# A graph layer on one core: the last 64 features' products made whole-array beside zeros, the mask product dropped, the order tables redrawn

## The chip, the core and the metric

The kernel runs on one core of a Trainium2 chip, in one launch. The metric is the device time in microseconds (us). Five engines each work through a list of their own, in order, and meet by semaphores: TensorE (PE) makes matrix products into eight PSUM banks, VectorE (DVE) and ScalarE (ACT) read PSUM, GpSimd (POOL) works in SBUF alone, and SyncE (SP) issues DMAs.

## What is computed

128 graphs of 128 nodes with 64 features. Layer 0, the costly one, sums over each node's neighbours a ReLU of 192 hidden features; layer 1 is a dense message and gate step. Both end in a layer norm.

```
mask = (adj > 0)                                  # 128 graphs, 128 x 128
xj_proj = x @ W1a
h = relu(xj_proj[:, :, None, :] + (x[:, :, None, :] - x[:, None, :, :]) @ W1b + b1)
hm = einsum('bjkh,bjk->bjh', h, mask)             # 192 hidden features
x = layernorm(x + hm @ W2 + deg * b2)             # layer 0
m = relu(relu(x @ W1g + b1g) @ W2g + b2g)
msg = relu(adj @ m)
r, z, n = gates(msg @ W_ih, x @ W_hh)
x = layernorm(x + (1 - z) * n + z * x)            # layer 1
```

## The kernel before

The mask is sparse, about one neighbour in ten. A node's neighbours are taken one after the other, in up to 18 places. Four graphs are one quad; there are 32 quads, q = 0 to 31. For a quad the features of the nodes, projected, lie in three PSUM banks as running pre-activations: banks 0 and 1 hold hidden features 0 to 127 of the four graphs, bank 2 holds features 128 to 191 of two graphs above each other, 64 partitions each. One round moves every node from its present neighbour to the next: PE adds the difference by a product of V (the neighbours' features, fp16, as stationary operand: VA for the first half of the sources, VB for the second) with a step matrix of -1, 0 and 1 in 8 bits (DM, columns = nodes), and DVE then adds the ReLU of the three banks to the sum AC in one SCALAR_TENSOR_TENSOR. A quad has nine rounds on VA (A1 to A9, PE's `round_a`, DVE's L1154) and nine on VB (B1 to B9, `round_b`, DVE's L1174). Rounds 1 to 6 cover 192 columns a graph, 7 and 8 cover 128, 9 covers 80. Places that a node does not use would count the ReLU of its last state too often; the surplus (NNB) that the start value is multiplied with takes that out.

Time step t runs the A rounds of quad t and the B rounds of quad t - 1 in turn: B1, A1, B2, A2, ... B9, A9. A and B use different banks (0 to 2 and 3 to 5), so PE can prepare one while DVE reads the other. A round is eight products on PE: four whole-array ones (`wide`, L841, stationary 128 x 128) and four with 64 stationary columns (`paired`, L850), of which those for partitions 0 to 63 and 64 to 127 run beside each other. `round_b` does `paired` first, `round_a` does `wide` first. B1 also has "leave", the closing product of the A rounds.

Everything else of the kernel is cut into pieces and put between the rounds by hand. The pieces are: p, the preparation of quad t + 1 (`ov`, `rank_t` L749, `rank_ov` L757 to L767, `words` L1120, `x_turn` L780, `v` L792 to L798, `v_low` L804, `v_out` with its DMAs L1777, `surplus` L813 and L816); r, the ranks of a group of eight graphs (`mask` L1688, `rank_n` L728, `split_x`, `count` L1584 to L1603, `off` L735 and, on DVE, SI L1111); t, the tail of quad t - 2 (`s_ov` L912, `out0` L923 to L941); n, d and e, the steps of layer 1 of a group (L609 to L712; its second product m2 is L655 and L658). s are the seeds (L827 and L833, then ACT's `ini` L1517 and POOL's start value, L1735, for which A1 waits), 0 to 3 the unpacking of step matrices on DVE (L1130), c clears AC. The tables ORDER (steps 1 to 30, one row for even and one for odd t), FIRST (t = 0) and LAST (t = 31, 32) say which pieces stand behind which round: a row has 19 places, place 0 ahead of B1, then one behind each B round and one behind each A round. All engines follow the same tables, each with its share of a piece. POOL waits at an unpacking until DVE has done it before it goes on with what stands behind it in the table. The pieces other than rounds use banks 6 and 7 in turn.

Counting of places (`count`) is done by POOL, from the ends of the ranks: NV, N12 = 6 NV and NVC. `surplus` adds on PE the column sums of the mask (L813) and NVC, transposed by a product with the identity (L816).

## Time and profile before

| | us |
|---|---|
| median of 3 runs (899.65 to 905.23) | 900.1 |
| the profiled execution | 907.5 |
| its span, first to last instruction | 905.7 |
| mean granted TensorE clock in it | 0.97 |

| engine | busy us | share | instructions |
|---|---|---|---|
| PE | 818.9 | 90% | 10240 |
| DVE | 795.6 | 88% | 880 |
| ACT | 622.5 | 69% | 1863 |
| POOL | 455.0 | 50% | 534 |

The span is the time from the first to the last instruction of one profiled execution; the runs are timed without the profiler. PE's busy time is the union of its products, whose ends are modelled, so it is not PE at its peak. An fp32 product stands in the trace as two, so L658 x8 are four products of the program. In the timeline a row merges equal instructions that follow each other (x4), its time is from the first's start to the last's end, and what stands in brackets is how long the engine was idle before it and what ended that. DVE's instructions overlap the next one's start a little. The chain that ended last runs over PE for 61% and DVE for 11% of the span.

### The profile page before, as it was taken

The page shows a single profiled execution, that of the slowest core. Times are in us where ns is not written, and L with a number is a line of the kernel's source. Part 1 is how long each engine was busy: PE and PEld are TensorE (multiplying, and loading weights), DVE is VectorE, ACT ScalarE, POOL GpSimd, SP SyncE. Part 2 cuts the span into 40 slices and gives each one's busy share as a digit, 9 for nine tenths or more (in the row PEclk, how much of TensorE's full clock was granted, in tenths as well). Part 3 has the DMA queues.
Part 4 walks back from the last instruction along what each step waited for, and adds up shares of the span by engine and source line. Part 5 has one row for each costly group of instructions (what it writes and reads, how often), then busy time and mean ns, then how long its engine had stood idle before and what let it go on. Part 6 is the DMA issues. An engine that isn't in the chain of part 4 may idle for free.

```text
span 905.7 us, 25602 instructions
## 1 busy us (share of the span) xinstructions
PE 818.9 (90%) x10240; PEld 563.5 (62%) x10240; DVE 795.6 (88%) x880; ACT 622.5 (69%) x1863; POOL 455.0 (50%) x534
## 2 busy tenths in 40 slices
PE   3778989999999999999999999989999999989963
PEld 2446657666676757666676756666675766666642
DVE  5789989999999999999999989999999999978742
ACT  4624557686877868686876868687786868667651
POOL 4413133564737465564736465472746556353751
...
GB/s 128 86 73 49 82 20 48 84 48 77 49 94 31 75 55 48 96 44 81 48 95 19 69 74 49 90 35 94 44 66 52 49 94 48 43 48 31 1 13 25
DMA packets 31564, 53.35 MB, mean 59 GB/s; under 512 B 8273, under 2 KB 17105, under 8 KB 31441
## 3 DMA queue, kind: packets, MB, share of 16 engines
...
q14 instruction: 42, 0.34, 0.1%
...
## 4 chain that ended last, share of the span: by engine, by line
PE 61%; issue 14%; DVE 11%; SPq 4%; DMA 3%; POOL 3%; ACT 2%; POOLq 0%; DVEq 0%
PE PS L841 16%; PE PS L850 11%; DVE AC L1174 5%; PE PS L924 4%; DVE AC L1154 3%; PE PS L912 2%; DMA VB<-VN 2%; PE PS L934 2%; DVE DM L1130 2%; PE PS L658 2%; PE PS L827 2%; PE PS L669 2%; PE PS L609 1%; POOL AC L1735 1%; PE PS L618 1%
## 5 line engine op out<-in xcount | busy, mean ns | idle before, releaser
L1174 DVE SCALAR_TENSOR_TENSOR AC<-PS,AC 128x1152 f32<-128x1152 f32 (+2 forms) x279 | 330.5, 1185 | 33.2 <-PE PS L841 30.9
L1154 DVE SCALAR_TENSOR_TENSOR AC<-PS,AC 128x1152 f32<-128x1152 f32 (+2 forms) x279 | 330.7, 1185 | 30.5 <-PE PS L850 24.9
L841 PE MATMUL PS<-DM,VA 128*128 128x192 fp8e5 (+1 forms) x1024 | 122.1, 243 | 20.1 <-DVE AC L1154 11.6
L841 PE MATMUL PS<-DM,VB 128*128 128x192 fp8e5 (+1 forms) x1024 | 123.6, 244 | 0.5 <-DVE AC L1171 0.5
L1735 POOL TENSOR_TENSOR AC<-AC,NNB 128x512 f32<-128x512 f32 x64 | 63.7, 1015 | 97.0 <-ACT AC L1517 84.4
L841 PEld LDWEIGHTS PS<-DM,VA 128*128 128x128 f16 x1024 | 77.5, 100 | 46.3 <-DVE AC L1154 34.3
L850 PE MATMUL PS<-DM,VB 128*64 128x192 fp8e5 (+1 forms) x1024 | 86.8, 248 | 21.3 <-DVE AC L1174 20.0
L841 PEld LDWEIGHTS PS<-DM,VB 128*128 128x128 f16 x1024 | 68.8, 98 | 35.0 <-issue 1.2
L850 PE MATMUL PS<-DM,VA 128*64 128x192 fp8e5 (+1 forms) x1024 | 88.6, 254 | 0.1
L1130 DVE TENSOR_SCALAR DM<-CW 128x1536 uint16<-128x1536 uint16 (+1 forms) x132 | 80.1, 655 | 3.4 <-DMA CW<-WM 3.4
L850 PEld LDWEIGHTS PS<-DM,VB 128*64 128x64 f16 x1024 | 41.9, 109 | 60.8 <-issue 34.0
L1688 POOL TENSOR_SCALAR MT<-AT 128x1024 bf16<-128x1024 f32 x15 | 41.9, 2794 | 72.0 <-DVE DM L1130 52.3
L1487 ACT ACTIVATE XE<-PS 128x512 f16<-128x512 f32 x64 | 37.8, 592 | 38.4 <-PE PS L781 38.4
L850 PEld LDWEIGHTS PS<-DM,VA 128*64 128x64 f16 x1024 | 36.3, 108 | 37.7 <-issue 30.5
L1728 POOL MEMSET AC<- 128x768 f32 x32 | 23.6, 738 | 71.8 <-PE PS L941 71.2
L1467 ACT ACTIVATE AM<-PS 64x512 int16<-64x512 f32 x64 | 37.9, 592 | 21.4 <-PE PS L749 21.0
L1724 POOL TENSOR_TENSOR SHL<-SO,SHL 128x256 f16<-128x256 f32 x31 | 20.9, 674 | 54.0 <-ACT SHL L1525 53.9
L1493 ACT ACTIVATE VN<-PS 128x384 f16<-128x384 f32 x64 | 31.1, 485 | 22.5 <-PE PS L798 22.5
L924 PE MATMUL PS<-w2s,AC 128*128 128x64 f32 x256 | 41.1, 293 | 0.0
L1498 ACT ACTIVATE VN<-PS 128x384 f16<-128x384 f32 x64 | 31.3, 490 | 13.9 <-PE PS L804 13.9
L912 PE MATMUL PS<-w2s,AC 128*64 128x64 f32 x1024 | 37.6, 228 | 0.0
L924 PEld LDWEIGHTS PS<-w2s,AC 128*128 128x128 f32 x256 | 37.5, 195 | 0.0
...
## 6 DMA issues: line engine op xcount, KB each, us to landing
CW<-WM SPq DMA_DIRECT2D x128, 160.0 KB, 2.8
...
VA<-VN SPq DMA_DIRECT2D x64, 96.0 KB, 2.2
VB<-VN SPq DMA_DIRECT2D x64, 96.0 KB, 2.2
...
```

Source lines behind the costliest of these rows:

```text
L841: last = e.matmul(PS[:, b + i % 2, 256 * (i // 2) + cols.start:256 * (i // 2) + cols.stop], lhs[:, GRAPH[i], 0:128], d[:, i, :], start=Fal ...
L850: last = e.matmul(PS[h, b + 2, 256 * (i // 2) + cols.start:256 * (i // 2) + cols.stop], lhs[:, GRAPH[i], 128:H], d[:, i, :], start=False, ...
L912: last = e.matmul(PS[64 * h:64 * h + 64, b, 64 * i:64 * i + 64], ac[:, n, c:c + 64], w2s[:, w, :], start=(w == 0), stop=(w > 0))
L924: e.matmul(o, ac[:, i % 2, 256 * (i // 2) + 64:256 * (i // 2) + 192], w2s[:, 0, :], start=False, stop=True, skip_group_check=True)
L1130: e.tensor_scalar(DM[m][:, halves], CW[t % 3][:, halves, first], 6 - 2 * m, 0xC0C0, ALU.logical_shift_left, ALU.bitwise_and).then_inc(s["d ...
L1154: e.scalar_tensor_tensor(dst, tiles(PS[:, b:b + 3, :])[:, :, cols], 0.0, dst, ALU.max, ALU.add).then_inc(s["sx"], 1)
L1174: e.scalar_tensor_tensor(dst, tiles(PS[:, b:b + 3, :])[:, :, cols], 0.0, dst, ALU.max, ALU.add).then_inc(s["sy"], 1)
L1467: e.activation(graphs(am[k])[:, :, 64 - 64 * h:192 - 64 * h], src[k], ACT.Copy, scale=2.0, bias=-258.0)
L1487: e.activation(XE[q % 4][:, 2 * k:2 * k + 2, :].rearrange("p i n -> p (i n)"), PS[:, b, :], ACT.Copy).then_inc(s["xe"], 1)
L1498: e.activation(VN[q % 2][:, 1, 2 * k:2 * k + 2, :], PS[:, b, :].rearrange("p (a n) -> p a n", a=2)[:, :, 0:H], ACT.Copy).then_inc(s["vl"], 1)
L1688: e.tensor_scalar(MT[g % 3][:], AT[g % NA][:], 0.0, None, ALU.is_gt).then_inc(s["mask"], 1)
L1735: e.tensor_tensor(t[:, h, nat], t[:, h, nat], NNB[q % 2][:, h, :], ALU.mult).then_inc(s["im"], 1)
```

## The change

Three things. First, `paired` becomes `padded`: the stationary operand of the products for the last 64 features is 128 columns wide, 64 of features and 64 of zeros, so the product writes all 128 partitions of the bank and adds zero to the other graph's half. VN, VA and VB get 256 places a graph instead of 192, with zeros behind the 192, set once by POOL; for every second graph the features are stored with the last 64 first, so that `left` and `right` find 128 features, or 64 beside 64 zeros, in a row of memory. For that `v` cuts its products for these graphs in two (64 and 128 columns). The copies of `v` go to every second graph. The DMAs of VA and VB move 128 KB instead of 96. The seeds keep their 64-column products.

Second, `surplus` loses the product over the mask: GpSimd's count takes the number of neighbours from the ends of the ranks, which it has in CT, into NVC, and ACT adds the constant as a bias.

Third, ORDER, FIRST and LAST are new throughout. DVE's and ACT's instructions for a piece are the same as before.

```
-    ("2ps3ee", "t", "", "pp", "", "ed", "dre", "t", "rtpp", "tc", "erdeee", "", "pdr", "p", "e", "pp", "rp", "", "0e1"),
-    ("d2sp3", "pp", "", "t", "dpe", "t", "pe", "pcttn", "n", "lpd", "d", "p", "d", "d0", "d", "p", "rdddp", "", "p1"),
+    ("s2p", "p", "pe3ee", "td", "erp", "t", "tt", "rpr", "p", "ed", "p", "epree", "pee", "d", "pce", "", "", "0", "r1"),
+    ("s2", "p3dp", "t", "", "d", "p", "eptp", "e", "ptl", "tp", "ndcpn", "d", "p", "dr", "pnd", "", "dd", "d", "01p"),
...
+        def left(t, i):
+
+            return t[:, i, 64 * (i % 2):64 * (i % 2) + 128]
+
+        def right(t, i):
+
+            c = 256 * i + 128 - 192 * (i % 2)
+            return t.rearrange("p i n -> p (i n)")[:, c:c + 128]
...
             def v(q, k, b, gates):
+                o = PS[:, b, :].rearrange("p (j n) -> p j n", j=2)
+                pieces = ((0, H, 0),) if k == 0 else ((0, 64, 128), (64, H, 0))
+                for c, d, f in pieces:
+                    e.matmul(o[:, :, c:d], on1[:], br[:, f:f + d - c].unsqueeze(1).to_broadcast([128, 2, d - c]), start=True, stop=True,
+                             skip_group_check=True)
                 for j in range(2):
                     x = XE[q % 4][:, 2 * j + k, nat]
+                    for w in (wxh, wxl):
+                        for c, d, f in pieces:
+                            last = e.matmul(o[:, j, c:d], x, w[:, 1, f:f + d - c], start=False, stop=True, skip_group_check=True)
...
             def surplus(q, b, gates):
-                mt = MT[g % 3][:, c:c + 4, :]
-                e.matmul(PS[:, b, :], on1[:], mt.rearrange("p (k a) n -> p a k n", a=2), start=True, stop=False)
                 for i in range(4):
                     m = c + GRAPH[i]
                     last = e.matmul(PS[:, b, 128 * i:128 * i + 128], NVC[g % 2][:, m:m + 1].to_broadcast([128, 128]),
-                                    idb[:], start=False, stop=(i == 3))
+                                    idb[:], start=True, stop=True)
...
-            def paired(q, lhs, d, cols):
+            def padded(q, lhs, d, cols):
 
                 b = 3 * (q % 2)
                 for i in range(4):
-                    h = slice(64 * (i % 2), 64 * (i % 2) + 64)
-                    last = e.matmul(PS[h, b + 2, 256 * (i // 2) + cols.start:256 * (i // 2) + cols.stop],
-                                    lhs[:, GRAPH[i], 128:H], d[:, i, :], start=False, stop=True, skip_group_check=True)
+                    last = e.matmul(PS[:, b + 2, 256 * (i // 2) + cols.start:256 * (i // 2) + cols.stop],
+                                    right(lhs, i), d[:, i, :], start=False, stop=True, skip_group_check=True)
...
-                e.activation(nnb[:, 0:512], PS[:, b, :], ACT.Copy)
+                e.activation(nnb[:, 0:512], PS[:, b, :], ACT.Copy, bias=-2.0 * C0)
...
-                e.tensor_tensor(NVC[i][:], cs[:, CSL + 1:CSL + 2].to_broadcast([128, GB]), N12[i][:, :, 0], ALU.subtract).then_inc(s["nvc"], 1)
+                e.tensor_tensor(CT[:], CT[:], N12[i][:], ALU.subtract).then_inc(s["nvc"], 1)
                 en.wait_ge(s["nvc"], 2 * g + 1)
-                e.tensor_tensor(NVC[i][:], NVC[i][:], N12[i][:, :, 1], ALU.subtract).then_inc(s["nvc"], 1)
+                e.tensor_tensor(NVC[i][:], CT[:, :, 0], CT[:, :, 1], ALU.add).then_inc(s["nvc"], 1)
...
             def setup():
+                for t in VN:
+                    e.memset(t[:].rearrange("p h i n -> p (h i) n")[:, :, H:256], 0.0)
```

What the tables do is best seen in the engines' lists. On PE, at the boundary of an even step to an odd one (t = 10 to 11), behind the last A9 product, before (L813 and L816 surplus, L655 and L658 m2, L827 and L833 seeds, L742 ov, then leave and B1):

```order
L813 MATMUL PS<-MT,on 128x512
L816 MATMUL PS<-idb,NVC 128x128 x4
L655 MATMUL PS<-br,on 128x512
L658 MATMUL PS<-BD,M 128x128 x4
L827 MATMUL PS<-XE,wxh 128x256 x4
L827 MATMUL PS<-XE,wxl 128x256 x4
L833 MATMUL PS<-XE,wxh 64x256 x4
L833 MATMUL PS<-XE,wxl 64x256 x4
L742 MATMUL PS<-SI,shf 128x512
L841 MATMUL PS<-CW,VA 128x128 x4
L850 MATMUL PS<-CW,VA 64x128 x4
L850 MATMUL PS<-DM,VB 64x192 x4
```

The same place in the changed kernel (there L850 is `wide` and L858 is `padded`, L743 is off, L825 surplus, L836 and L842 the seeds, L750 ov, L663 and L666 m2):

```order
L743 MATMUL PS<-NV,tri 128x16
L825 MATMUL PS<-idb,NVC 128x128 x4
L836 MATMUL PS<-XE,wxh 128x256 x4
L836 MATMUL PS<-XE,wxl 128x256 x4
L842 MATMUL PS<-XE,wxh 64x256 x4
L842 MATMUL PS<-XE,wxl 64x256 x4
L850 MATMUL PS<-CW,VA 128x128 x4
L858 MATMUL PS<-CW,VA 128x128 x4
L858 MATMUL PS<-DM,VB 128x192 x4
L850 MATMUL PS<-DM,VB 128x192 x4
L750 MATMUL PS<-SI,shf 128x512
L663 MATMUL PS<-br,on 128x512
```

The mask product is gone, m2 and ov have moved behind B1, off has come to stand ahead of the surplus, and only the seeds still change the tiling.

On DVE at the same boundary, from B9 to A1, before (L1174 are B rounds, L1154 A rounds, L1130 the unpacking; SI, L1111, is ahead of B9):

```order
L1111 TENSOR_TENSOR SI<-iot,VE 128x1024
L1174 SCALAR_TENSOR_TENSOR AC<-PS,AC 128x6x80
L1154 SCALAR_TENSOR_TENSOR AC<-PS,AC 128x6x80
L1130 TENSOR_SCALAR DM<-CW 128x1536 x4
L1174 SCALAR_TENSOR_TENSOR AC<-PS,AC 128x6x192
L1154 SCALAR_TENSOR_TENSOR AC<-PS,AC 128x6x192
```

And now (L1182 are B rounds, L1162 A rounds, L1138 the unpacking, L1119 SI):

```order
L1182 SCALAR_TENSOR_TENSOR AC<-PS,AC 128x6x80
L1138 TENSOR_SCALAR DM<-CW 128x1536
L1162 SCALAR_TENSOR_TENSOR AC<-PS,AC 128x6x80
L1119 TENSOR_TENSOR SI<-iot,VE 128x1024
L1138 TENSOR_SCALAR DM<-CW 128x1536 x2
L1182 SCALAR_TENSOR_TENSOR AC<-PS,AC 128x6x192
L1138 TENSOR_SCALAR DM<-CW 128x1536
L1162 SCALAR_TENSOR_TENSOR AC<-PS,AC 128x6x192
```

SI has moved behind A9, and the four unpackings are spread from B9 to A1.

## Rows read from the trace of the kernel before

**Rows 1.** Windows, one pair of steps: length, each engine's busy time, clock, DMA.

```profile
409.02:460.29 51.27, 49.27 (x640) 34.15 (x639) 47.94 (x47) 39.21 (x119) 28.99 (x34) 1.00 0.24 63
```

**Rows 2.** Waits of DVE, 100 to 790 us: total, times, longest.

```profile
DVE AC L1174 <- PE PS L841: 22.9, 39, 1.3
DVE AC L1154 <- PE PS L850: 19.7, 48, 1.7
```

**Rows 3.** Timeline of DVE at two boundaries: start, us, what, idle before it.

```profile
406.06 1.96 DVE L1130 TENSOR_SCALAR DM<-CW 128x1536 uint16<-128x1536 uint16 x4
409.02 1.36 DVE L1174 SCALAR_TENSOR_TENSOR AC<-PS,AC 128x1152 f32<-128x1152 f32 x1 [1.00 <-PE PS L841]
410.67 1.36 DVE L1154 SCALAR_TENSOR_TENSOR AC<-PS,AC 128x1152 f32<-128x1152 f32 x1 [0.29 <-PE PS L850]
...
431.46 2.56 DVE L1130 TENSOR_SCALAR DM<-CW 128x1536 uint16<-128x1536 uint16 x3
434.29 1.36 DVE L1174 SCALAR_TENSOR_TENSOR AC<-PS,AC 128x1152 f32<-128x1152 f32 x1 [0.26 <-PE PS L841]
436.20 1.36 DVE L1154 SCALAR_TENSOR_TENSOR AC<-PS,AC 128x1152 f32<-128x1152 f32 x1 [0.56 <-POOL AC L1735]
```

**Rows 4.** Timeline of DVE within steps.

```profile
419.51 1.36 DVE L1154 SCALAR_TENSOR_TENSOR AC<-PS,AC 128x1152 f32<-128x1152 f32 x1 [0.43 <-PE PS L850]
...
437.48 1.35 DVE L1174 SCALAR_TENSOR_TENSOR AC<-PS,AC 128x1152 f32<-128x1152 f32 x1
438.74 1.35 DVE L1154 SCALAR_TENSOR_TENSOR AC<-PS,AC 128x1152 f32<-128x1152 f32 x1
...
445.34 0.81 DVE L1120 TENSOR_TENSOR WM<-c,AM 128x1280 uint16<-128x1280 uint16 x1
...
452.30 0.96 DVE L1154 SCALAR_TENSOR_TENSOR AC<-PS,AC 128x768 f32<-128x768 f32 x1
...
455.07 1.22 DVE L1111 TENSOR_TENSOR SI<-iot,VE 128x1024 bf16<-128x1024 bf16 x1
456.20 0.65 DVE L1174 SCALAR_TENSOR_TENSOR AC<-PS,AC 128x480 f32<-128x480 f32 x1
```

**Rows 5.** Timeline of PE, A1 and B2 of an even step.

```profile
435.26 0.50 PE L841 MATMUL PS<-DM,VA 128*128 128x192 fp8e5 x4
435.70 0.36 PE L850 MATMUL PS<-DM,VA 128*64 128x192 fp8e5 x4
435.89 0.33 PE L850 MATMUL PS<-DM,VB 128*64 128x192 fp8e5 x4
436.15 0.50 PE L841 MATMUL PS<-DM,VB 128*128 128x192 fp8e5 x4
436.49 0.38 PE L749 MATMUL PS<-MT,trt 128*128 128x512 bf16 x1
```

**Rows 6.** Timeline of PE from A9 to B1, boundary of an even to an odd step.

```profile
404.45 0.39 PE L813 MATMUL PS<-MT,on 128*128 128x512 bf16 x1
404.68 0.39 PE L816 MATMUL PS<-idb,NVC 128*128 128x128 bf16 x4
...
406.01 0.60 PE L827 MATMUL PS<-XE,wxh 128*128 128x256 f16 x4
...
408.48 0.50 PE L841 MATMUL PS<-DM,VB 128*128 128x192 fp8e5 x4
```

**Rows 7.** Timeline of POOL, start value of the even step.

```profile
434.10 1.98 POOL L1735 TENSOR_TENSOR AC<-AC,NNB 128x512 f32<-128x512 f32 x2 [0.96 <-DVE DM L1130]
```

**Rows 8.** Timeline of POOL and DVE, start of the kernel.

```profile
8.36 0.72 POOL L1674 TENSOR_SCALAR be<-bs 128x192 f32<-128x192 f32 x1 [4.21 <-DMA bs<-in_b2g]
...
64.52 0.56 DVE L1130 TENSOR_SCALAR DM<-CW 128x1536 uint16<-128x1536 uint16 x1 [0.89 <-DMA CW<-WM]
```

**Rows 9.** The page: a group of weight loads, and the DMAs of VA.

```profile
L841 PEld LDWEIGHTS PS<-DM,VA 128*128 128x128 f16 x1024 | 77.5, 100 | 46.3 <-DVE AC L1154 34.3
VA<-VN SPq DMA_DIRECT2D x64, 96.0 KB, 2.2
```

More of the change, by code:

```diff
@@ L51 @@
 CSL = CIO + 64
-CML = CSL + 2
+CML = CSL + 1
 CMR = CML + 128
@@ L98, in constants @@
     c[:, CSL] = less
-    c[:, CSL + 1] = 2.0 * less - 2.0 * C0
     c[0, CML:CML + 128] = -C1
@@ L255, in build @@
         CW = [sb(f"CW{i}", [128, 2, 1280], U16) for i in range(3)]
-        VN = [sb(f"VN{i}", [128, 2, 4, H], F16) for i in range(2)]
-        VA = [sb(f"VA{i}", [128, 4, H], F16) for i in range(3)]
-        VB = [sb(f"VB{i}", [128, 4, H], F16) for i in range(3)]
+        VN = [sb(f"VN{i}", [128, 2, 4, 256], F16) for i in range(2)]
+        VA = [sb(f"VA{i}", [128, 4, 256], F16) for i in range(3)]
+        VB = [sb(f"VB{i}", [128, 4, 256], F16) for i in range(3)]
         XE = [sb(f"XE{i}", [128, 4, 256], F16) for i in range(4)]
@@ L877, in round_a @@
                     pe.wait_ge(s["sx"], 9 * q + n - 1)
-                last = wide(q, VA[q % 3], d, cols)
+                last = wide(q, VA[q % 3][:], d, cols)
                 if q == 0:
@@ L881, in round_a @@
                     pe.wait_ge(s["sx"], n - 1)
-                paired(q, VA[q % 3], d, cols).then_inc(s["gx"], 1)
+                padded(q, VA[q % 3][:], d, cols).then_inc(s["gx"], 1)
             def round_b(q, n):
@@ L888, in round_b @@
                     leave = lasts(q, 0, 0)
-                    wide(q, VA[q % 3], leave, nat)
-                    paired(q, VA[q % 3], leave, nat)
+                    wide(q, VA[q % 3][:], leave, nat)
+                    padded(q, VA[q % 3][:], leave, nat)
                 elif q == NQ - 1:
@@ L894, in round_b @@
                     pe.wait_ge(s["sy"], 9 * q + n - 1)
-                last = paired(q, VB[q % 3], d, cols)
+                last = padded(q, VB[q % 3][:], d, cols)
                 if q == NQ - 1:
@@ L1504, in surplus @@
                 nnb = NNB[q % 2][:].rearrange("p i n -> p (i n)")
-                e.activation(nnb[:, 0:512], PS[:, b, :], ACT.Copy)
+                e.activation(nnb[:, 0:512], PS[:, b, :], ACT.Copy, bias=-2.0 * C0)
                 for a in range(2):
                     h = slice(64 * a, 64 * a + 64)
-                    last = e.activation(nnb[h, 512:768], PS[h, b, 256 * a:256 * a + 256], ACT.Copy)
+                    last = e.activation(nnb[h, 512:768], PS[h, b, 256 * a:256 * a + 256], ACT.Copy, bias=-2.0 * C0)
                 last.then_inc(s["nnc"], 1)
```

30 lines of the change are left out of this document (13 added, 17 removed).

## The prediction

> **What bounds the kernel now.** I read the windows first. Between about 50 and 850 us the kernel repeats a pair of time steps, an odd one from the B1 at 409.02 to that at 434.29 and an even one to 460.29, 51.27 us together. In it TensorE (PE) is busy 49.27 us and VectorE (DVE) 47.94 [rows 1]: neither is plainly the bound, and PE's busy time is modelled from matmuls that overlap, so it can't be taken at its word. The waits of DVE say more: from 100 to 790 us, 13.5 such pairs, it stood 42.6 us (22.9 + 19.7) for products of PE [rows 2]. The timeline says where: B1 and A1, just behind the step boundary, wait 1.00 and 0.29 us in one step, 0.26 and, for GpSimd (POOL), 0.56 in the other [rows 3]; within a step mostly A4, 0.43 [rows 4]. Other rounds start 1.26 apart, which is what DVE itself needs: 1.35, less 0.09 of overlap [rows 4]. So DVE is to be fed, and PE, which works in order, is late for it at a few places.
>
> What PE's time goes into is seen in its timeline [rows 5]. From four whole-array products of 192 columns to whole-array work it is 0.34 us (436.15 to 436.49), 0.083 each. The same four ahead of 64-column ones take 0.44 (435.26 to 435.70). Four 64-column ones run two beside each other: 0.19 to the next such four, 0.26 to whole-array ones. Each change of tiling costs about 0.10 us, and PE was not waiting there for anything else.
>
> **The change, part by part.** All sums are for one pair of steps; counts are from PE's instruction list.
>
> *Padding.* The paired products become whole-array products beside zeros: four slots a group instead of two. 24 groups of 192 columns add 2 x 0.083 each, 4.0; eight of 128 and the two closing ones (leave) 2 x 0.056, 1.1; four of 80 columns 2 x 0.035, 0.3 (0.056 and 0.035 are 0.083 scaled by columns). That is +5.4 us. Against it the changes of tiling fall from 72 to 14: 58 x 0.10 = -5.8. The product over the mask (L813) goes, 0.23 each (404.45 to 404.68) [rows 6], -0.45. Cutting every second V into 64 + 128 columns adds five instructions a step and no columns, some 0.02. PE's own work goes from 47 to 45.7, hardly more than -1 us. Were half of a switch hidden, it would rise by 1.5 or so instead; I take the full price, since the row shows PE going from one group right to the next.
>
> The Trainium skill, "TensorEngine Tiling (Array Packing)", Key Properties, says that changing the tiling mode drains TensorE, which the 0.10 agrees with. Its Theoretical Speedup gives two 64-column tiles up to 2x, and that speaks against this change: by it alone the pair gets 5.4 us of PE work more, some 78 us in all.
>
> *The order tables.* DVE needs, for a pair, 24 x 1.26 + 8 x 0.87 + 4 x 0.57 for rounds, 8 x 0.48 for unpacking steps (L1130, 1.96 for four [rows 3]), 1.13 for SI and 2 x 0.73 for WM, each its row less the overlap [rows 4]: 46.0. Of the 5.3 us more that it takes, 1.1 is that three L1130 last 2.56 where POOL works, against 1.47 [rows 3]; the rest is waiting. More than 5.3 can't be gained. I go through the pair with the new lists and the rows' durations: a round of 192 columns needs 0.67 on PE, starts 0.05 after DVE frees its bank, and 0.21 pass from its last slot to DVE (B1: 408.48, 0.34 of slots, 409.02 [rows 6]).
>
> Even to odd, zero at B9's end (before: 405.49, the 0.57 of A9 ahead of 406.06). Before, surplus, the m2 products (L655, L658) and a switch stand ahead of the seeds, which begin at 406.01, +0.52 [rows 6]. Now 0.25 us of work does, and seeds begin at +0.05, right behind B9. Seeds 0.87, switch and second part 0.55, switch and leave 0.56, B1 0.67: issued by 2.69, so DVE could start at 2.90. But DVE has B9, A9, SI and three L1130 in its list and comes at 3.13: B1 no longer waits. m2, ov and rank_t (1.54) follow, then A1: DVE has it at 5.10 (0.23 late), one more L1130 done on the way. Before, A1 came 5.18 after B9 [rows 3], with SI outside.
>
> Odd to even: surplus, seeds, ov, leave and B1 are issued by 2.91, DVE starts B1 at 3.12, some 1.1 idle (before 434.29 - 430.89 = 3.40, B9's end again 0.57 ahead of the L1130 at 431.46). A1 follows at 4.39, if its start value is there: before, POOL's two products began 0.96 late behind an L1130 [rows 7] for which the new list no longer holds them, so 5.31 (436.20 - 430.89) - 0.96 = 4.35 is possible.
>
> Between: from A1 to the end of B9 DVE has eleven rounds of 1.26, four of 0.87, B9 0.57 and WM 0.73, 18.7. Odd step: A1's issue ends at 4.89, the s_ov products 0.93, two switches and B2 0.67 make 6.70, DVE 6.91 against 6.37: 0.53 late. In the same way A3, B6, A6 and B8 are late by 0.08, 0.10, 0.04 and 0.30. A4 is not, as its 1.24 of fillers are split between A3 and B5. So 5.10 + 18.7 + 1.05 = 24.9. Even step: the fourth L1130 stands here, nothing is late: 4.39 + 18.7 + 0.48 = 23.6. Together 48.5; fp32 fillers ran about 0.1 over their slots and there are three: 48.8. The pair goes from 51.3 to 48.8, **-2.5 us**. Steps 2 to 30 are 14.5 pairs: -36. Later pairs of before ran 0.25 longer than this one on average, from A1's waits; half of that, -2.
>
> *Taken as nothing.* Two memsets of VN on POOL (about 0.5 each, an estimate from the zeroing of others of that size) lie ahead of 4.21 us in which POOL waits for the biases [rows 8]; without that cover, 1. VA and VB grow by a third: 2.2 us to landing [rows 9] may become 2.9, but v_out is issued a round (1.76) earlier; uncovered, 0.7 a step, 20. GpSimd's counting has nine instructions before and after, ScalarE's bias adds none. *Start:* step 1 stood 0.89 for a CW behind 30 weight loads on SP's queue [rows 8]; that L1130 now comes after A9: -1. Last two steps: 0, within 3, since their tables are new and a chain of layer-1 work that the change leaves alone ends the kernel.
>
> Sum: -39. The profiled run took 907.5 us (span 905.7), so 868.5; the median of the runs shown is 7.4 lower, which gives **861 us**.
>
> **Rivals.** *The start value sets A1.* ScalarE's two copies and POOL's two products lie between seeds and A1. If A1 of the even step stays 5.3 behind B9, 0.9 a pair is lost: 1.6 x 14.5 = 23, 875 with start and later pairs. For it: the 0.56 wait [rows 3]. Against: 0.96 of it is a hold that goes. 0.16. *Nearly all waiting goes:* 47.7 a pair, so -52: 847. It needs two engines with 45.7 and 46.0 us of work to interlock almost without loss. 0.11. *Padded weight loads show:* LDWEIGHTS takes 0.1 [rows 9]; at that pitch all padded products add 3.8 a pair, PE needs 49.5, 1.5 is gained: 878. Against: the whole-array groups load the same 128 columns at 0.083. 0.03. The Trainium skill, "TensorE: Matmul & The Clock Gate", Back-to-back issue gap, has about 81 ns for load and product of 128 columns; here even 192 columns take 0.083. *No change:* a late round only moves, as each group waits for the round before; under 0.6 a pair: 893 to 905. 0.06. *Slower, the count ahead of the seeds:* L743 waits for nv from POOL and now stands ahead of surplus, seeds, leave and B1, where L735 stood before B9. DVE's SI needs it too. By the boundary above some 3 us late cost nothing, 5.5 eat the gain; with three more stretches of POOL's work like that of [rows 7] (5.9) and their handovers in front, 0.7 a pair is lost: 910. Against: POOL's list has the same work between mask and count as before. 0.04.
>
> **Chances.** Forecast 0.60 (850 to 872), then 0.16, 0.11, 0.03, 0.06, 0.04. The range 845 to 884 leaves out the last two and tails. Within 1% (9 us) the runs of this kernel (899.65 to 905.23) hardly tell a change from none. Faster by over 1%: 0.60 + 0.16 + 0.11 + 0.03 = 0.90; within 0.06; slower 0.04.
>
> **What would show it.** A pair of 48.8 (47.7 to 50); groups of padded products 0.34 apart and 14 changes of tiling; no wait at B1 of odd steps, about 1.0 at B1 of even ones, 0.5 at B2 of odd ones. Wrong if padded groups take more, if A1 waits for L1735, if PE waits at L743 or L757, or if L1130 lasts over 1 us again.

## The result, and the profile after the change

| | before | after |
|---|---|---|
| median, us | 901.3 (899.65 to 905.23, 4 runs) | 877.9 (874.1 to 877.97, 4 runs) |
| ratio, with its 95% interval | | 0.9724 (0.9681 to 0.9767) |
| the profiled execution: time, span | 907.5, 905.7 | 877.9, 876.3 |

The kernel is 2.8% faster, by about 25 us. The forecast was 861 us with a range of 845 to 884: the sign and the range hold, and the size, 40 us, was put too high by about 15.

A pair of steps in the trace of the changed kernel, an odd step from the B1 at 398.37 to that at 423.69 and an even one to 448.35, shows what became of [rows 1]. The columns are the window, its length, each engine's busy time with its instructions, the granted clock, and the DMA share and rate.

```profile
core 0: us, PE busy (x) PEld busy (x) DVE busy (x) ACT busy (x) POOL busy (x), PEclk, DMA share, GB/s
398.37:423.69 25.32, 25.16 (x331) 20.95 (x332) 23.51 (x25) 18.77 (x58) 11.19 (x10) 1.00 0.33 90
423.69:448.35 24.66, 22.75 (x316) 19.12 (x316) 24.66 (x25) 19.31 (x61) 18.20 (x25) 1.00 0.21 50
398.37:448.35 49.98, 47.91 (x646) 40.07 (x648) 48.17 (x49) 38.08 (x119) 29.39 (x34) 1.00 0.27 70
```

The pair went from 51.27 to 49.98 us; 48.8 was forecast. The two halves differ: in the odd step PE is busy nearly all the time, in the even one DVE is. Next come DVE's waits from 100 to 790 us. Before the change it waited 42.6 us for PE there [rows 2], and 4.2 more for POOL, by the first line; the other three lines are from after the change:

```profile
DVE AC L1154 <- POOL AC L1735: 4.2, 7, 0.9
...
DVE AC L1182 <- PE PS L850: 21.6, 40, 1.0
DVE AC L1162 <- PE PS L858: 0.6, 1, 0.6
DVE AC L1162 <- POOL AC L1745: 0.4, 2, 0.2
```

So 46.8 us of waiting became 22.6: for PE 22.2 instead of 42.6, for POOL 0.4 instead of 4.2. The places are as they should be: the waits at A1, A4 and B9 went. But DVE's own busy time in the pair is 48.17, against 47.94 before. The timeline of DVE (start, duration, what, and idle time before it, where there is some) shows both boundaries from B1 on, and the instruction that grew:

```profile
398.37 1.34 DVE L1182 SCALAR_TENSOR_TENSOR AC<-PS,AC 128x1152 f32<-128x1152 f32 x1
399.64 1.05 DVE L1138 TENSOR_SCALAR DM<-CW 128x1536 uint16<-128x1536 uint16 x1
400.62 1.34 DVE L1162 SCALAR_TENSOR_TENSOR AC<-PS,AC 128x1152 f32<-128x1152 f32 x1
402.32 1.36 DVE L1182 SCALAR_TENSOR_TENSOR AC<-PS,AC 128x1152 f32<-128x1152 f32 x1 [0.36 <-PE PS L850]
...
421.18 1.51 DVE L1138 TENSOR_SCALAR DM<-CW 128x1536 uint16<-128x1536 uint16 x3
423.69 1.36 DVE L1182 SCALAR_TENSOR_TENSOR AC<-PS,AC 128x1152 f32<-128x1152 f32 x1 [0.99 <-PE PS L850]
424.97 1.36 DVE L1162 SCALAR_TENSOR_TENSOR AC<-PS,AC 128x1152 f32<-128x1152 f32 x1
...
427.97 1.35 DVE L1162 SCALAR_TENSOR_TENSOR AC<-PS,AC 128x1152 f32<-128x1152 f32 x1
429.24 1.90 DVE L1128 TENSOR_TENSOR WM<-c,AM 128x1280 uint16<-128x1280 uint16 x1
431.06 1.34 DVE L1182 SCALAR_TENSOR_TENSOR AC<-PS,AC 128x1152 f32<-128x1152 f32 x1
```

B1 and A1 at both boundaries behave as forecast (no wait at B1 of the odd step; 0.99 at that of the even one; none at its A1, where POOL's 0.56 stood in [rows 3]). But the shift that makes WM took 1.90 us, and 0.82 in [rows 4]. What POOL did meanwhile, from its timeline:

```profile
427.83 1.27 POOL L1653 TENSOR_TENSOR GT<-XG,GN 128x512 f32<-128x512 f32 x1 [1.77 <-ACT GN L1403]
429.18 1.27 POOL L1656 TENSOR_TENSOR GT<-GT,GZ 128x512 f32<-128x512 f32 x1
430.42 1.25 POOL L1734 TENSOR_TENSOR SHL<-SO,SHL 128x256 f16<-128x256 f32 x1
```

L1656, a product of layer 1's gate, had begun 0.06 us ahead of WM and runs to 430.45; WM ends at 431.14, 0.69 behind that. L1734, which is next on POOL and takes 0.67 elsewhere (below), takes 1.25 here and ends at 431.67, 0.53 behind WM. From the times it looks as if WM could not go on before POOL's instruction was done, and POOL's next one not before WM was. The rounds, fp32 with one operand in PSUM, keep their 1.35 under such a POOL instruction (the one at 427.97 runs under L1653). Grouped by form over 150 to 770 us (busy time in us and the mean of one in ns stand behind the bar), this is, before:

```profile
L1130 DVE TENSOR_SCALAR DM<-CW 128x1536 uint16<-128x1536 uint16 x99 | 62.3, 682 | 0.0
L1120 DVE TENSOR_TENSOR WM<-c,AM 128x1280 uint16<-128x1280 uint16 x24 | 19.6, 815 | 0.0
```

and after:

```profile
L1138 DVE TENSOR_SCALAR DM<-CW 128x1536 uint16<-128x1536 uint16 x97 | 58.2, 629 | 0.0
L1128 DVE TENSOR_TENSOR WM<-c,AM 128x1280 uint16<-128x1280 uint16 x25 | 32.9, 1315 | 0.0
```

By the means, at equal counts, unpacking gained about 5 us and WM lost about 12: in all 13 even steps in which L1656 runs, WM has met it. The old tables had put WM where POOL was idle. The new ones moved it, for the even steps, from 11.05 us behind B1 (445.34 in [rows 4], B1 at 434.29) to 5.55 (429.24, B1 at 423.69).

### The profile page after: what moved, and what is told of

It is laid out like the page before. It is cut to its first block, busy times and chain, and to the rows that moved or that the text cites. A ratio compares the mean times of both kernels' runs of the same rounds, so it can differ in the third digit from the quotient of the medians.

```text
span 876.3 us, 25828 instructions
## 1 busy us (share of the span) xinstructions
PE 786.3 (90%) x10335; PEld 651.6 (74%) x10368; DVE 803.6 (92%) x880; ACT 606.7 (69%) x1863; POOL 462.1 (53%) x536
## 4 chain that ended last, share of the span: by engine, by line
PE 51%; issue 28%; DVE 16%; ACT 2%; POOL 1%; DMA 1%; SPq 1%; POOLq 0%; DVEq 0%
PE PS L850 12%; PE PS L858 11%; DVE AC L1182 8%; DVE AC L1162 4%; PE PS L836 2%; PE PS L932 2%; PE PS L920 2%; PE PS L677 2%; PE PS L842 2%; PE PS L666 2%; PE PS L617 1%; PE PS L618 1%; PE PS L620 1%; PE PS L629 1%; PE PS L627 1%
## 5 line engine op out<-in xcount | busy, mean ns | idle before, releaser
L1182 DVE SCALAR_TENSOR_TENSOR AC<-PS,AC 128x1152 f32<-128x1152 f32 (+2 forms) x279 | 329.4, 1181 | 26.6 <-PE PS L850 25.1
L1162 DVE SCALAR_TENSOR_TENSOR AC<-PS,AC 128x1152 f32<-128x1152 f32 (+2 forms) x279 | 329.4, 1180 | 4.9 <-PE PS L858 2.9
L850 PE MATMUL PS<-DM,VA 128*128 128x192 fp8e5 (+1 forms) x1024 | 121.5, 241 | 17.2 <-DVE AC L1162 11.1
L858 PE MATMUL PS<-DM,VB 128*128 128x192 fp8e5 (+1 forms) x1024 | 120.6, 240 | 17.9 <-DVE AC L1182 15.0
L850 PE MATMUL PS<-DM,VB 128*128 128x192 fp8e5 (+1 forms) x1024 | 119.8, 240 | 0.5 <-DVE AC L1179 0.5
L858 PE MATMUL PS<-DM,VA 128*128 128x192 fp8e5 (+1 forms) x1024 | 120.3, 240 | 0.1
L850 PEld LDWEIGHTS PS<-DM,VA 128*128 128x128 f16 x1024 | 77.7, 99 | 47.8 <-DVE AC L1162 30.4
L1745 POOL TENSOR_TENSOR AC<-AC,NNB 128x512 f32<-128x512 f32 x64 | 66.1, 1053 | 85.7 <-DVE DM L1138 51.4
L858 PEld LDWEIGHTS PS<-DM,VB 128*128 128x128 f16 x1024 | 75.6, 98 | 43.4 <-issue 18.8
L858 PEld LDWEIGHTS PS<-DM,VA 128*128 128x128 f16 x1024 | 83.5, 98 | 0.9 <-DVE AC L1159 0.6
L850 PEld LDWEIGHTS PS<-DM,VB 128*128 128x128 f16 x1024 | 83.4, 98 | 0.9 <-DVE AC L1179 0.9
L1138 DVE TENSOR_SCALAR DM<-CW 128x1536 uint16<-128x1536 uint16 (+1 forms) x132 | 79.2, 628 | 2.5 <-DMA CW<-WM 2.5
L1738 POOL MEMSET AC<- 128x768 f32 x32 | 23.6, 739 | 66.9 <-PE PS L949 66.2
L1734 POOL TENSOR_TENSOR SHL<-SO,SHL 128x256 f16<-128x256 f32 x31 | 28.5, 918 | 49.7 <-ACT SHL L1533 49.7
L1540 ACT ACTIVATE XR<-PS 128x256 f32<-128x256 f32 x32 | 12.3, 384 | 48.5 <-PE PS L949 48.5
L1430 ACT ACTIVATE YO<-Y,st 128x64 f32<-128x64 f32 x120 | 31.8, 337 | 16.3 <-POOL st L1633 16.3
L1128 DVE TENSOR_TENSOR WM<-c,AM 128x1280 uint16<-128x1280 uint16 x32 | 39.7, 1240 | 2.0 <-ACT OT L1489 2.0
```

The lines of the kernel that those rows point to most:

```text
L850: last = e.matmul(PS[:, b + i % 2, 256 * (i // 2) + cols.start:256 * (i // 2) + cols.stop], left(lhs, i), d[:, i, :], start=False, stop=Tr ...
L858: last = e.matmul(PS[:, b + 2, 256 * (i // 2) + cols.start:256 * (i // 2) + cols.stop], right(lhs, i), d[:, i, :], start=False, stop=True, ...
L1128: e.tensor_tensor(WM[q % 2][:], c7[:], AM[q % 2][:].bitcast(U16), ALU.logical_shift_left).then_inc(s["wm"], 1)
L1138: e.tensor_scalar(DM[m][:, halves], CW[t % 3][:, halves, first], 6 - 2 * m, 0xC0C0, ALU.logical_shift_left, ALU.bitwise_and).then_inc(s["d ...
L1162: e.scalar_tensor_tensor(dst, tiles(PS[:, b:b + 3, :])[:, :, cols], 0.0, dst, ALU.max, ALU.add).then_inc(s["sx"], 1)
L1182: e.scalar_tensor_tensor(dst, tiles(PS[:, b:b + 3, :])[:, :, cols], 0.0, dst, ALU.max, ALU.add).then_inc(s["sy"], 1)
```

## The experiments

All are edits of the changed kernel, run with the kernel before beside them. Step lengths are from B1 to B1 in the timelines, between steps 8 and 27; where no range is given it is the usual length, and in several kernels one to three of these steps are longer, by up to 1.5 us. "Ratio" is to the kernel before.

| kernel | odd step | even step | median us | ratio (95%) |
|---|---|---|---|---|
| before | 25.27 | 26.0 to 27.15 | 901.3 | 1 |
| the change | 25.32 | 24.66 | 877.9 | 0.9724 (0.9681 to 0.9767) |
| e_oldtab | 25.23 | 25.50 to 27.25 | 898.1 | 0.9968 (0.9952 to 0.9985) |
| e_paired | 25.98 | 24.69 | 895.6 | 0.9933 (0.9908 to 0.9957) |
| e_mask | 25.63 | 24.77 | 881.7 | 0.9790 (0.9759 to 0.9820) |
| e_oldlast | 25.31 | 24.65 | 880.3 | 0.9751 (0.9713 to 0.9789) |
| e_words5 | 25.25 | 24.09 | 868.1 | 0.9639 (0.9609 to 0.9669) |
| e_words6 | 25.22 | 24.11 | 870.1 | 0.9642 (0.9607 to 0.9677) |
| e_unpack_even | 25.22 | 24.03 | 870.6 | 0.9651 (0.9618 to 0.9685) |
| e_unpack_both | 25.16 | 24.02 | 869.3 | 0.9647 (0.9613 to 0.9681) |
| e_hold | 25.22 | 24.51 | 874.2 | 0.9691 (0.9656 to 0.9727) |
| e_hold_unpack | 25.22 | 24.44 | 873.0 | 0.9674 (0.9636 to 0.9712) |
| e_hold_paired | 25.92 | 24.64 | 894.4 | 0.9903 (0.9866 to 0.9940) |
| e_gz | 25.29 | 23.96 | 865.7 | 0.9620 (0.9593 to 0.9646) |

### The parts of the change, one at a time

**e_oldtab**: the padded products and the new count under the old tables (ORDER, FIRST and LAST as in the minus lines of the diff).

> The changed kernel (padded products, counting by GpSimd) with all order tables as before the change: what padding and the dropped product are worth without new tables. Theory of the prediction: padding takes 58 changes of tiling of 0.10 us out of a pair of steps and puts 5.4 us of slots in, the product over the mask goes too, so PE has 1 us less work, of which DVE sees at most that: 886 to 898 us, likeliest 892; most of the gain (2.5 us of a pair) is the tables'. Rival, padding itself is the gain: 880 or less. Rival, half of a change of tiling was hidden behind the products, so padding makes PE's work longer: 903 or more.

898.1, 0.3% below the kernel before, at the far end of what the prediction's theory gave. Odd steps stayed at 25.23. In even ones the quiet steps gained 0.5, but some are up to 1.8 longer. The waits of PE, 100 to 790 us, show what goes with it, first before the change, then here:

```profile
PE PS L841 <- DMA VB<-VN: 3.1, 5, 1.2
```

```profile
PE PS L850 <- DMA VB<-VN: 6.5, 6, 1.7
```

With the old tables PE waits now and then for the DMA that brings VB; a third more bytes (128 KB for 96 an issue) and a PE that comes earlier go with the 6.5 us; no run parts the two. Under the new tables, in the change and in e_gz, PE has no such wait from 100 to 790 us. The longer even steps from 20 on of the kernel before (26.32 to 27.15 instead of 26.0, in steps 20 to 28) are these 3.1 us. I had put them down to A1, where they come to light.

**e_paired**: the new tables and count, with the old products.

```diff
-            last = e.matmul(PS[:, b + 2, 256 * (i // 2) + cols.start:256 * (i // 2) + cols.stop],
-                            right(lhs, i), d[:, i, :], ...)
+            h = slice(64 * (i % 2), 64 * (i % 2) + 64)
+            c = 128 - 128 * (i % 2)
+            last = e.matmul(PS[h, b + 2, 256 * (i // 2) + cols.start:256 * (i // 2) + cols.stop],
+                            lhs[:, i, c:c + 64], d[:, i, :], ...)
```

> The changed kernel with the last 64 features' products again as two 64-column products side by side, all else (tables, counting, layout of VA and VB) kept. Theory of the prediction: 5.4 us of slots go and about 58 changes of tiling of 0.10 us come back in a pair, 0.4 more work on PE, and where nothing else stands between rounds the new changes delay a round by 0.05 to 0.1, mostly into waits that DVE has already: 880 to 888 us. Rival, padding is neutral and the tables are all: 876 to 879. Rival, the 64-column pairs win since the changes hide: 870 or less.

895.6: 19 us by the ratios more than the change, and 880 to 888 was expected. Neither half of the change is worth much without the other: the new products and count under the old tables bring 0.3% (e_oldtab), the new tables and count with the old products 0.7%; together they bring 2.8%. Two things are seen in the trace. The odd step is 0.66 longer, 9 us over 14 steps. Rows of PE, A2 of an even step, show why the two forms are so close:

```profile
336.24 0.50 PE L850 MATMUL PS<-DM,VA 128*128 128x192 fp8e5 x4
336.67 0.36 PE L860 MATMUL PS<-DM,VA 128*64 128x192 fp8e5 x4
336.96 0.40 PE L736 MATMUL PS<-trt,MT 128*128 128x128 bf16 x4
```

The whole-array four take 0.43 and the side-by-side four 0.29 to the next, 0.72, and the padded form 0.66 to 0.68 (in the change, from 401.44 to 402.12):

```profile
401.44 0.50 PE L858 MATMUL PS<-DM,VB 128*128 128x192 fp8e5 x4
401.79 0.49 PE L850 MATMUL PS<-DM,VB 128*128 128x192 fp8e5 x4
402.12 0.49 PE L850 MATMUL PS<-DM,VA 128*128 128x192 fp8e5 x4
```

The other is TensorE's clock. Four times between 130 and 820 us it stood at 1.2 GHz (0.50 granted) instead of 2.4 for 3.4 us, as in the second window here:

```profile
350.60:354.00 3.40, 2.49 (x34) 1.40 (x32) 3.40 (x5) 2.27 (x13) 2.57 (x6) 1.00 0.03 8
354.00:357.40 3.40, 3.40 (x27) 2.34 (x29) 3.40 (x6) 2.69 (x9) 0.52 (x1) 0.50 0.64 146
```

The seeds then run at half speed and B1 comes 1.4 to 1.5 late:

```profile
358.94 1.36 DVE L1184 SCALAR_TENSOR_TENSOR AC<-PS,AC 128x1152 f32<-128x1152 f32 x1 [1.37 <-PE PS L850]
```

All four times it was the stretch just ahead of an odd step's B1. Four times 1.4 are 6 us. In the first 130 us, with more such stretches, this execution falls another 5 behind (mean granted clock 0.91 there, 0.96 in the change); but it is the slowest of the ten, 900.6 us, 5 above their median. The mean granted clock of the ten runs was 0.968 to 0.979, that of the change 0.984 to 0.986.

What lowers the clock there is open. Ahead of the fall, in the rounds of 128 and 80 columns, PE had been busy 2.49 of 3.40 us. But it was so at the same place of the nine other boundaries of this kind from step 7 on, where the clock stayed up; the first line below is one of them. And the same place of the change, in the second line, has PE busy for less, 2.34, and the clock up as well:

```profile
299.92:303.32 3.40, 2.49 (x35) 1.40 (x32) 3.40 (x5) 2.27 (x13) 2.57 (x6) 1.00 0.06 13
...
341.57:344.97 3.40, 2.34 (x35) 1.61 (x33) 3.40 (x5) 2.28 (x13) 2.64 (x6) 1.00 0.05 13
```

The Trainium skill, "TensorE: Matmul & The Clock Gate", Part 1, has activity release the throttle. PE's busy time alone does not bear that out here; whether a product on half the columns counts for less than one beside zeros is a guess that no run tests. What the runs show is only that the falls between 130 and 800 us come in the two kernels that have pairs under the new tables, and in none of the padded ones, nor in the kernel before.

**e_mask**: the product over the mask is back in front of surplus, with the old count.

```diff
+                mt = MT[g % 3][:, c:c + 4, :]
+                e.matmul(PS[:, b, :], on1[:], mt.rearrange("p (k a) n -> p a k n", a=2), start=True, stop=False)
...
-                                    idb[:], start=True, stop=True)
+                                    idb[:], start=False, stop=(i == 3))
```

> The changed kernel with the unused places counted as before: the product over the mask (0.23 us on PE) is back in front of the four surplus products, and GpSimd's count and ScalarE's bias are as before the change. Theory of the prediction: surplus stands ahead of the seeds, so B1 of even steps, which waits for PE, comes 0.23 later, and at B1 of odd steps the same 0.23 is about covered by SI and three unpackings on DVE; 0.23 to 0.4 a pair, so 880 to 883 us. Rival, the product was covered: 876 to 878. Rival, GpSimd's new count was what set something: under 874.

881.7, in the range of the prediction's theory. The product is 0.23 us on PE, twice a pair, and the pair is 0.42 longer: both land nearly in full on the path. The even step's B1 now waits 1.23 (0.99 in the change at the same step):

```profile
424.13 1.36 DVE L1185 SCALAR_TENSOR_TENSOR AC<-PS,AC 128x1152 f32<-128x1152 f32 x1 [1.23 <-PE PS L853]
```

At the odd B1, where I had expected 0.2 us of cover, it comes 0.13 late (398.50 and 398.37, behind a B9 at the same time within 0.01), and the wait at B2 grows by another 0.13. So the cover was about 0.1.

**e_oldlast**: only LAST as before.

> The changed kernel with the old table for the last two time steps (LAST) alone. Theory of the prediction: the end is a chain of layer-1 work that the tables don't shorten, so the time stays within 3 us of the changed kernel's 876 to 878. Rival, the new LAST brought the 2.6 us that the stretch behind the B1 of step 31 got shorter, and something of step 30: 881 or more.

880.3 against 877.9, by the ratios 0.3% with overlapping intervals, so the times alone don't tell them apart. In the traces step 30 is 26.56 instead of 25.46 and the stretch behind it 1.7 longer, so new LAST is worth 2 to 3 us, just inside what the prediction allowed.

### WM moved: where most of the missing 15 us are

**e_words5**: WM of even steps one round later, with the rest of the lists kept.

```diff
-    (..., "td", "erp", "t", "tt", ...
+    (..., "td", "er", "pt", "tt", ...
```

> The changed kernel with one letter of its table for even steps moved: the 16-bit shift that makes WM (L1128) stands one round later in every engine's list, behind B3 instead of behind A2. Theory collision: in the changed kernel this instruction begins in even steps while GpSimd is 0.3 us into a product (L1656) and takes 1.90 us instead of 0.82, and DVE has nothing to spare there, so each even step is 1.1 us longer. One round later it would begin about 0.35 us ahead of the end of GpSimd's next, shorter operation, so it takes about 1.1, even steps go from 24.65 to 23.9 us, and the whole to about 867 us (864 to 870). Rival, TensorE sets the even step: DVE's late start only uses up slack, WM gets shorter, but DVE then waits for PE by as much, and the time stays within 2 us of 876 to 878.

868.1, 8 to 10 us less than the change. WM takes 1.27, 0.63 less than at its old place, and even steps are 0.57 shorter. In the usual step it begins 0.59 us ahead of L1734's end. The timelines of DVE and, one fence on, of POOL, are from step 14, where it begins 0.30 ahead and took 0.97:

```profile
375.34 0.97 DVE L1128 TENSOR_TENSOR WM<-c,AM 128x1280 uint16<-128x1280 uint16 x1
```

```profile
374.96 0.68 POOL L1734 TENSOR_TENSOR SHL<-SO,SHL 128x256 f16<-128x256 f32 x1
375.58 1.75 POOL L1710 TENSOR_TENSOR X1l<-X,SQ 128x512 f16<-128x512 f32 x1
```

L1734 ends at 375.64 and WM at 376.31, again 0.67 behind it; now L1710 is the one held up, 1.75 instead of 1.16.

**e_words6**: two rounds later ("erp", "t", "tt" becomes "er", "t", "ptt").

> The changed kernel with WM of even steps (L1128) two rounds later than in the change, behind A3. In the run with it behind B3 it still took 1.28 us, beginning 0.29 ahead of the end of GpSimd's L1734, and held up L1710. Theory collision: behind A3 it begins at the end of L1710, 0.0 to 0.25 us ahead of it, so it takes 0.82 to 1.05, even steps go from 24.1 to 23.75 and the whole to 863 us (861 to 866). Rival, with WM out of the way PE is the next bound of even steps: 867 to 869, the same as one round later, and waits of DVE for PE appear in the even step's rounds.

WM is at 0.81, and the step still takes 24.11: the first rival. A3 waits 0.25 for PE:

```profile
428.06 1.36 DVE L1162 SCALAR_TENSOR_TENSOR AC<-PS,AC 128x1152 f32<-128x1152 f32 x1 [0.25 <-PE PS L858]
429.33 0.81 DVE L1128 TENSOR_TENSOR WM<-c,AM 128x1280 uint16<-128x1280 uint16 x1
```

Ahead of A3 stand 1.1 us of fillers on PE (L931 and L932). At its place in the change WM gives PE the time for them. So the table had put it there to good use, and the loss was only that it met L1656.

**e_unpack_even** and **e_unpack_both**, both on top of e_words6: the fourth unpacking of the even step into B1's wait ("s2p", "p", "pe3ee" becomes "s23p", "p", "peee"), then also that of the odd step from B1 to A1 ("p3dp", "t" becomes "pdp", "3t").

> As e_words6, and in even steps the fourth unpacking (L1138, for DM3) stands ahead of B1 instead of behind A1. DVE waits 0.95 us for PE at that B1, and the unpacking lasts 0.47. Theory of the prediction (DVE is bound in even steps once it is fed): the wait falls to 0.48, the 0.47 behind A1 goes, and even steps get up to 0.47 shorter: up to 6.5 us less than e_words6, 857 to 861 us. Rival, PE bounds the first rounds of the even step: B2 comes no earlier, the wait only moves from B1 to B2, and the time is that of e_words6 within 1.5 us.

> As e_unpack_even, and in odd steps the fourth unpacking stands behind A1 instead of behind B1, where it took 1.05 us, since it began 0.09 us into GpSimd's second product on the start values (L1745). Theory collision: behind A1 it takes 0.55, A1 begins when the start value is there, about 0.3 us earlier, and the 0.36 of waiting at B2 takes up part of it; 0.1 to 0.35 a pair, so 1.5 to 5 us less than e_unpack_even. Rival, GpSimd's products set A1 in odd steps: A1 begins as late as before behind an idle DVE, the unpacking then delays B2: no gain or up to 4 us more than e_unpack_even.

870.6 and 869.3: no gain that can be measured. The wait at B1 halves (0.54), and A2 takes it over, with some at A3: PE has seeds, leave and the first rounds with over 2 us of fillers in a row there. In the odd step the unpacking is at 0.55 again, but A1 starts only 0.21 us earlier (2.03 behind B1), behind a wait of 0.69 for PE; the unpacking then stands behind A1, B2 starts at 3.79 in both kernels, and the step gets 0.06 shorter. So the unpacking of 1.05 costs next to nothing. The rows are from the even step, B1 and A2:

```profile
420.56 1.36 DVE L1182 SCALAR_TENSOR_TENSOR AC<-PS,AC 128x1152 f32<-128x1152 f32 x1 [0.54 <-PE PS L850]
...
424.77 1.36 DVE L1162 SCALAR_TENSOR_TENSOR AC<-PS,AC 128x1152 f32<-128x1152 f32 x1 [0.18 <-PE PS L858]
```

### GpSimd moved instead of WM

**e_hold**: one wait more, on POOL ahead of L1656, and all lists as in the change.

```diff
                 po.wait_ge(s["gd"], 3 * u + 1)
+                po.wait_ge(s["wm"], min(2 * u + 8, NQ))
                 po.wait_ge(s["sig"], 2 * u + 2)
```

> The changed kernel with one wait more and no list changed: GpSimd's product L1656 waits until WM of the same even step (L1128 on DVE) is made. In the changed kernel L1656 begins 0.3 us ahead of WM, which then takes 1.90 us instead of 0.82, in 13 even steps. With WM moved one or two rounds on, even steps took 24.1, and I read two different remainders in that: 0.46 of the collision still there (one round), and a wait of 0.33 at A3 for fillers on PE that WM no longer covered (two rounds). Theory: at its place and at 0.82, WM still covers those fillers, GpSimd starts 1.2 us later and has the time, so even steps take 23.6 and the whole 862 us (860 to 864). Rival, PE bounds even steps at 24.1 wherever WM stands: 867 to 870, as in the runs with WM moved. Rival, GpSimd's chain is late for what follows (L717, seeds): 870 or more, with waits for POOL or late A1.

WM takes 0.82 and A3 does not wait, but a form of the second rival came in its stead: B4 waits, which takes back 0.75 of the 1.08 us that WM gave, and the step is only 0.15 shorter. DVE, then POOL:

```profile
426.90 0.82 DVE L1128 TENSOR_TENSOR WM<-c,AM 128x1280 uint16<-128x1280 uint16 x1
...
428.90 1.35 DVE L1162 SCALAR_TENSOR_TENSOR AC<-PS,AC 128x1152 f32<-128x1152 f32 x1
430.91 1.36 DVE L1182 SCALAR_TENSOR_TENSOR AC<-PS,AC 128x1152 f32<-128x1152 f32 x1 [0.67 <-PE PS L850]
```

```profile
427.84 1.27 POOL L1657 TENSOR_TENSOR GT<-GT,GZ 128x512 f32<-128x512 f32 x1 [1.07 <-issue]
429.08 0.67 POOL L1735 TENSOR_TENSOR SHL<-SO,SHL 128x256 f16<-128x256 f32 x1
```

L1735 (L1734 of the change) stands behind the held product; PE needs its SHL for L949, ahead of B4. A wait holds everything that is queued behind it, which I had not asked of this one.

**e_hold_unpack** and **e_hold_paired**, on top of it:

> As e_hold, and in even steps the fourth unpacking stands ahead of B1, in DVE's wait there of 0.95 us, instead of behind A1. With WM moved, this gave 0.08 us an even step, since waits of 0.26 at A2 and 0.20 at A3 took its place. Theory, PE's work between seeds and A3 bounds there: 0 to 0.15 a step, 0 to 2 us less than e_hold. Rival, WM in its place covers A3 again, so 0.2 to 0.4 a step: 3 to 6 us less.

> As e_hold, with the last 64 features' products as two 64-column products side by side, as in e_paired, where odd steps got 0.66 us longer and even ones, with the slowed WM, only 0.03, and TensorE's clock stood at half for 3.4 us four times in mid-run, 1.4 us each. Theory, WM hid what pairing costs in even steps: here they are 0.3 to 0.7 longer than in e_hold, and the kernel 22 to 30 us slower than e_hold (884 to 892). Rival, even steps have slack on PE either way: they stay at e_hold's length, and the kernel is 13 to 20 us slower than e_hold.

The first gave 0.07 a step, as the theory that PE bounds there has it. The second is 20 us slower than e_hold: odd steps 0.70 longer, even ones 0.13 and not 0.3 to 0.7. So even steps do have slack on PE for most of what the paired form costs; it is the rival with its 13 to 20 us that fits, with four stretches at half clock in mid-run again.

**e_gz**: L1656 behind the next L1734 in POOL's list, with no wait added. Nothing else moves on any engine.

```diff
             def gd(u):
                 ...
-                po.wait_ge(s["gd"], 3 * u + 1)
-                po.wait_ge(s["sig"], 2 * u + 2)
-                e.tensor_tensor(GT[:], GT[:], GZ[:], ALU.mult).then_inc(s["gd"], 1)
+                owed.append(u)
+
+            def gz():
+                for u in owed:
+                    po.wait_ge(s["gd"], 3 * u + 1)
+                    po.wait_ge(s["sig"], 2 * u + 2)
+                    e.tensor_tensor(GT[:], GT[:], GZ[:], ALU.mult).then_inc(s["gd"], 1)
+                owed.clear()
...
             def s_ov(q, b, gates):
                 ...
+                layer1["gz"]()
```

> The changed kernel with GpSimd's list alone changed: the product L1656 stands behind the next L1734 instead of ahead of it, with no added wait. In e_hold, WM at its place and at 0.82 let A3 begin with no wait, but L1734, queued behind the held L1656, came late for PE, and B4 waited 0.67 more. Here L1734 ends about 6.1 us behind B1 and WM begins 5.85 behind it, so WM takes 0.9 to 1.1, L1734 is 1.9 us earlier than in the change, and L1656 runs behind WM. Theory collision: even steps take 23.6 to 23.8 and the whole 862 to 865 us. Rival, PE bounds even steps at 24.1: 867 to 870, with waits at A3 or B4 by as much as WM is shorter. Rival, WM is served only after L1656 too, since GpSimd has its next operation at hand: 874 to 878, WM at 1.9 or more.

865.7 (865.04 to 870.76, 6 runs), the fastest of all, 1.1% below the change by the ratios. DVE, then POOL:

```profile
421.16 1.19 DVE L1128 TENSOR_TENSOR WM<-c,AM 128x1280 uint16<-128x1280 uint16 x1
```

```profile
421.00 0.67 POOL L1742 TENSOR_TENSOR SHL<-SO,SHL 128x256 f16<-128x256 f32 x1
421.64 1.85 POOL L1662 TENSOR_TENSOR GT<-GT,GZ 128x512 f32<-128x512 f32 x1
```

WM meets the short L1742 (L1734 of the change) instead: 0.71 less than in the change, and the even step is 0.70 shorter. I had expected 0.9 to 1.1 for WM, as I took its start (5.85 behind B1) from step 14, where it is 0.3 later than in nearly all others (5.55); in step 14 of this run WM did take 0.88. In place, with its fillers covered and SHL in time, WM's time and the step's go one for one, and most of the missing part of the forecast lies there: 0.70 of the 1.08 us were taken back in this way, some 9 us over 13 steps. That the last 0.4 would follow was not tried.

## Why the prediction was right, and where it was off

**The bound.** DVE was late for want of PE, at few places, and it was freed there: its waits for PE fell from 42.6 to 22.2 us (100 to 790).

**Padding.** Four products to the next four take 0.33 to 0.35, as said, and that half of a switch might be hidden is not what the rows show. The net on PE was put at 0.4 us a pair; e_paired and e_hold_paired show 0.7 and 0.8 a pair on the path, nearly all in odd steps. Two times the speed from two 64-column tiles, which the Trainium skill, "TensorEngine Tiling (Array Packing)", Theoretical Speedup, gives as the most, did not decide: e_paired is 2.1% slower than the change by the ratios. What I left out is the clock, above. Padding, with the new count, is worth 2.9 us under the old tables, and padding alone 19 under the new ones. That the two parts need each other was in no sentence of the prediction. Two side sums were off, and nothing hung on them: 47 us of PE's work and the terms -0.8 make 46.2, not 45.7, and the rival of weight loads adds 4.4 a pair by its own pitch (24, 10 and 4 groups), not 3.8.

**The mask product.** -0.45 a pair forecast, 0.42 measured (e_mask).

**Even to odd.** From B9's end (395.24, its start 394.67 and the 0.57 pitch) seeds began 0.19 behind it (0.05 forecast), with 0.26 us of work in front:

```profile
395.17 0.17 PE L743 MATMUL PS<-NV,tri 128*128 128x16 bf16 x1
395.20 0.38 PE L825 MATMUL PS<-idb,NVC 128*128 128x128 bf16 x4
395.43 0.60 PE L836 MATMUL PS<-XE,wxh 128*128 128x256 f16 x4
```

DVE came to B1 at 3.13 (398.37), as forecast to the hundredth. A1 was forecast at 5.10 and is at 5.38 (400.62), since an unpacking fell under POOL's start value; without that (e_unpack_both) it was 0.21 earlier, and waited for PE.

**Odd to even.** B1 at 3.12 forecast, 3.23 measured, 0.99 of it idle; A1 at 4.39 forecast, 4.51 measured. The rival that the start value sets A1 fell.

**Late rounds of the odd step.** B2, A3, B6, A6, B8 were to be late by 0.53, 0.08, 0.10, 0.04 and 0.30; measured, as gap above the usual overlap, 0.44, 0.12, 0.20, 0.03 and 0.33, and A9 by 0.15, which I had not. 1.27 against 1.05. The forecast counted steps from B9's end to B9's end; so counted, the odd step came out at 25.2 and not 24.9, and the even one at 24.75 and not 23.6.

**DVE's own need: the step that failed.** The sum put 46.0 us for DVE in a pair, with every L1130 and WM at its undisturbed length, although it named the 1.1 us that three L1130 lost to POOL in [rows 3] and counted them as won. What the new order puts beside POOL's instructions was never looked at. I had the rule in the trace (2.56 us for three, [rows 3]) and used it for the old order only. The new one has one WM at 1.90, +1.08, and one L1138 at 1.05. The first is 1.08 of the 1.15 us by which the even step came late. e_words5 and e_gz show it giving back 0.57 of 0.63 and 0.70 of 0.71; e_words6 and e_hold, which take the whole 1.08 out, gave back only 0.55 and 0.15, since PE was late for something else there. The second cost 0.06 (e_unpack_both). That an unpacking would last over 1 us again stood among the signs of being wrong, and it came; the instruction that cost the time was the other one.

A cross-check stands in the run itself: layer 1 is not under way yet in steps 2 to 4, so L1656 isn't there. Those three took 73.6 us after and 77.8 before, 4.2 gained, where 1.5 pairs at 2.5 make 3.8, and step 4 took 23.64, which is the forecast for an even step. It is weak support, since PE has less to do there too and both executions had stretches at half clock. Steps 5 to 29, 12.5 pairs, took 626.0 after and 644.1 before: 1.45 a pair.

The Trainium skill states the rule outright: "SBUF — State Buffer", Who interferes with whom, has GpSimd share a pair of ports with VectorE, held for a whole instruction by whoever issues first, while the other fully blocks. It names `tensor_scalar` in two-port modes and `tensor_tensor` with both inputs in SBUF (L1138 and L1128 here), and exempts instructions with at most one SBUF input outside those modes (the rounds). The rows above agree, and so do L1734 and L1710, held up behind WM. One row does not: at the start of the kernel before, at 29.10, WM begins 0.28 us ahead of the end of POOL's one-input mask operation (L1688) and still takes 0.81. The rule should have been weighed.

**Start, end and the base.** Step 1 no longer waits for CW, but is no shorter in all; by the B1 of step 2 the gain is 0.1 us, and 1 was forecast. Step 30 gained 4.4 and the end 2.6 where 0 was forecast. 2 to 3 of that is the new LAST (e_oldlast); in step 30 the profiled execution of before had its clock at half for 6.8 us from 803.4 on. The mean clock of that execution was 0.970. In 44 others of the same kernel it was 0.972 to 0.985, and the four of them at 0.972 to 0.974 took 905.4 to 906.5 us; so it was slow by its clock. The 7.4 us taken off for the median were rightly taken off, but the 4.4 are part of them. From the median: 901.3, less 22.3 for steps 2 to 29 and 2 to 3 for the new LAST, is 876 to 877, with 877.9 measured.

**Later pairs.** Half of 0.25 us a pair was to be won, from A1's waits. All of it was, and most of it (2.9 of 3.8 us in steps 2 to 28) was the DMA of VB, ahead of A1. The prediction took the larger transfers as hidden, since v_out moved up a round; e_oldtab, without that move, shows 6.5 us of waits.

**The chances.** The likeliest case, 850 to 872 with 0.60, did not come. The time fell where the cases of 875 and 878 were put, by neither of their mechanisms. So that the range holds is owed to its width, and to rivals that were wrong: the bound, the freed places and the sign are as predicted, and the size is not. A rival "a DVE instruction meets POOL's", with 1.08 x 13 = 14 us, would have been at the place.
